# One transformer layer on one core: work moved at the seams of its four stages

## The chip, the cores and the metric

The kernel runs on one core of a Trainium2 chip. The metric is the device time of one launch in microseconds (us). The kernel before took 3391.18, 3396.15 and 3394.44 us in three runs, median 3394.44. The change is compared with it in the same way.

## The reference

Only the structure is shown; B = 2, S = 2048, D = 512, all float32.

```
x = x + LN(softmax(mask(LN(x) @ ctx.T / sqrt(512))) @ ctx) * gamma + beta     # ctx: 77 rows
y = LN(x)
src = rms(y + gqa(y)) * norm1       # 16 query heads, 4 key/value heads of 32, softmax over 2048 keys
src = src + moe(src)                # 8 experts, top 2, capacity 1280 rows, 512 -> 1024 -> gelu -> 512
out = x + rms(src) * norm2
```

## The kernel before

The 4096 rows are cut into 8 chunks of 512 rows (four tiles of 128). Four functions run one after the other, each with a block of its own; every engine ends its part before any starts the next block. Within a block each engine's instructions stand in a written order, and semaphores join them.

**Stage 1, `phase_project`.** For chunk c: layer norm of X, attention over ctx, x1 = X + that, y = LN(x1), then y transposed and projected to queries, keys and values. The chunks are staggered: while chunk c's attention runs, chunk c-1's y is transposed (`p_ps_t`, L559), split into a high part (ScalarE, `p_yTh`, L340) and a low part (VectorE, `p_yTl`, L482), and projected in six steps of twelve matmuls (L83 to L85). ScalarE takes each step's result as `p_hi` (L350) and VectorE as `p_lo` (L496). On VectorE `head_statistics(c + 2)` (four BATCH_NORM_STATS2, L399, four aggregates, L403, and the mask penalty `p_pen`, L415) stands at the end of `chunk(c)`, so `second_low(c)`, which makes `p_yTl`, comes behind it. GpSimd computes the reciprocal roots (L252, L254) and adds the rows `p_yb` (L277) and `p_xb` (L262).

**Stage 2, `phase_attend`.** 32 units (chunk, key/value head). A unit's keys and queries lie in `KS` and `QS`; for every unit the queries of the next chunk, the keys and the values are loaded. TensorE computes scores twice (once for the maxima, L1340, once transposed for the exponentials, L1354), GpSimd adds tiles of exponentials (L939, L943) so that fewer denominator matmuls (L1374) are needed. At the end of the last chunk its rows are projected, normalised (GpSimd L956, L951, then ScalarE L1095), transposed (L1392), routed to experts, and sent to `xe_d` by GpSimd's indirect DMAs (L1013).

**Stage 3, `phase_experts`.** SyncE loads an expert's w1 and w2 (into the space of `kept.x1`), ScalarE and VectorE split w1 into high and low parts (L1626, L1688), the rows' blocks are transposed (L1768) and go up and down. The results are added to `src_d` by indirect DMAs (L1610). At its end half of x1 is loaded.

**Stage 4, `phase_combine`.** Loads src and the rest of x1 on SyncE's queue. ScalarE sums squares (L1885), GpSimd makes the reciprocal root (L1870, L1872), VectorE multiplies (L1901, out of and into SBUF) and adds x1 (L1907); ScalarE stores `p_OUT` (L1878), of which there are two buffers.

Of the kernel before, what the change touches and what calls it, by code (L numbers as in the profile page):

```python
# [103 lines left out]
def phase_project(nc, x, ctx, mask, gamma, beta, qw, qb, kw, kb, vw, vb, ob, x1_d, y_d, qh_d, ql_d, kh_d, kl_d, v_d):  # L104
# [5 lines left out]
    with Scope(nc, "p1") as s:  # L110
# [283 lines left out]
        def _(dve):  # L394
# [104 lines left out]
            def chunk(c):  # L499
# [23 lines left out]
                if c + 2 < NC:  # L523
                    head_statistics(c + 2)
# [1430 lines left out]
```

## Time and profile before

| stretch | from, us | to, us |
|---|---|---|
| stage 1 | 0 | 341.1 |
| stage 2 | 341.1 | 2352.1 |
| stage 3 | 2352.1 | 3321.2 |
| stage 4 | 3321.2 | 3389.2 |

The profiled execution took 3391.0 us, its span is 3389.2 us. The ends of the stages are the first issues of SyncE in each block. In the whole span PE is busy 92%, DVE 63%, ACT 48%, POOL 60%, at a mean granted clock of 0.955; in stage 4 PE does nothing, and the sixteen DMA engines are busy 0.81 of the time. The shares of a whole span mix four stages that have different limits; what a change is worth is read in the stage that it touches, at the wait that ends last.

### The profile page before, as it was taken

The numbers are of one execution on the slowest core, as the hardware profiler recorded it, in microseconds if no ns is written. First come the engines' busy times: TensorE is split into PE (matmuls) and PEld (weight loads), VectorE is DVE, ScalarE is ACT, GpSimd is POOL, SyncE is SP. The second block draws the span as 40 slices with busy tenths as digits, with TensorE's granted clock in tenths as the row PEclk, the third lists the DMA queues.
The fourth block names the chain that finished last, engine by engine and source line by source line (L and its number), as shares of the span: only waits on it lengthen the run. The fifth ranks groups of instructions, "written<-read, shape, count | busy, mean of one in ns | idle before, by whom it ended". The sixth has DMA issues, their size and how long they took to land. (4 is left out here: it accounts for less than half of the span.)

```text
span 3389.2 us, 45574 instructions
## 1 busy us (share of the span) xinstructions
PE 3131.6 (92%) x16808; PEld 2017.8 (60%) x16808; DVE 2133.4 (63%) x3820; ACT 1616.5 (48%) x3252; POOL 2017.9 (60%) x856
## 2 busy tenths in 40 slices
PE   5888799999999999999999999983999999999990
PEld 4666444544544544544545445432999899989980
DVE  6765888878788788788788787822333333333325
ACT  2332166656566566556566565651333334333322
POOL 3332199889899899899899898993111111111112
PEclk7989599999999999999999999996999999999995
DMA  3544724212221313113122121002333333333237
GB/s 112 178 164 160 184 87 148 59 37 52 51 57 36 70 35 72 33 36 76 29 60 56 37 51 49 14 21 103 89 94 70 79 90 82 84 69 93 48 75 254
DMA packets 195376, 270.67 MB, mean 80 GB/s; under 512 B 80903, under 2 KB 86023, under 8 KB 192629
## 3 DMA queue, kind: packets, MB, share of 16 engines
q1 hardware_dynamic: 172864, 223.34, 22.9%
q0 software_dynamic: 16640, 35.42, 5.7%
q10 hardware_dynamic: 5685, 9.49, 0.8%
q8 instruction: 107, 1.75, 0.2%
q14 instruction: 80, 0.66, 0.1%
HBM read 152.98 MB, written 117.57 MB: 80 GB/s over the span
## 5 line engine op out<-in xcount | busy, mean ns | idle before, releaser
L1072 ACT ACTIVATE p_PR<-p_ps_b 128x512 f32<-128x512 f32 x2048 | 1066.1, 603 | 729.3 <-PE p_ps_b L1354 721.4
L1153 DVE TENSOR_REDUCE p_mxp<-p_ps_a 128x1 f32<-128x512 f32 x2048 | 1282.0, 681 | 209.3 <-PE p_ps_a L1340 198.6
L943 POOL TENSOR_TENSOR p_PP<-p_PP,p_PR 128x2048 f32<-128x2048 f32 x224 | 1027.5, 4587 | 38.2 <-ACT p_PR L1072 14.7
L1340 PE MATMUL p_ps_a<-p_KS,p_QS 96*128 96x512 f32 x2048 | 830.2, 437 | 36.3 <-DMA p_KS<-kh_d 15.9
L1354 PE MATMUL p_ps_b<-p_QS,p_KS 98*128 98x512 f32 x2048 | 755.7, 416 | 7.0 <-ACT p_PR L1072 6.0
L1340 PEld LDWEIGHTS p_ps_a<-p_KS,p_QS 96*128 96x128 f32 x2048 | 386.7, 192 | 472.8 <-DVE p_mxp L1153 325.2
L939 POOL TENSOR_TENSOR p_PP<-p_PR 128x2048 f32<-128x2048 f32 x128 | 587.0, 4586 | 96.3 <-ACT p_PR L1072 81.6
L1610 POOL DMA_INDIRECT src_d<-p_YE,p_token x80 | 123.9, 1548 | 836.9 <-DVE p_YE L1737 709.3
L1360 PE MATMUL p_ps_pv<-p_PR,p_VS 128*32 128x512 f32 x4096 | 511.3, 600 | 0.0
L1354 PEld LDWEIGHTS p_ps_b<-p_QS,p_KS 98*128 98x128 f32 x2048 | 387.4, 190 | 202.0 <-ACT p_PR L1072 117.5
L1655 ACT ACTIVATE p_hf<-p_ps_h 128x384 f32<-128x384 f32 (+1 forms) x256 | 112.0, 437 | 575.4 <-PE p_ps_h L85 569.4
L83 PE MATMUL p_ps_h<-p_xTh,p_w1h 128*128 128x256 f32 (+1 forms) x1024 | 323.6, 316 | 1.2 <-DVE p_xTl L1717 1.2
L85 PE MATMUL p_ps_h<-p_xTh,p_w1l 128*128 128x256 f32 (+1 forms) x1024 | 318.3, 311 | 0.0
L84 PE MATMUL p_ps_h<-p_xTl,p_w1h 128*128 128x256 f32 (+1 forms) x1024 | 318.1, 311 | 0.0
L1724 DVE TENSOR_TENSOR p_hl<-p_hf,p_hh 128x384 fp32r<-128x384 f32 (+1 forms) x256 | 126.1, 492 | 284.3 <-ACT p_hh L1659 284.3
L1737 DVE TENSOR_SCALAR p_YE<-p_ps_y,p_weight 128x512 f32<-128x512 f32 x80 | 60.0, 750 | 332.2 <-PE p_ps_y L85 278.6
L84 PE MATMUL p_ps_y<-p_w2l,p_hh 128*128 128x512 f32 x640 | 253.8, 397 | 0.0
L83 PE MATMUL p_ps_y<-p_w2h,p_hh 128*128 128x512 f32 x640 | 253.7, 396 | 0.0
L85 PE MATMUL p_ps_y<-p_w2h,p_hl 128*128 128x512 f32 x640 | 253.5, 396 | 0.0
L1360 PEld LDWEIGHTS p_ps_pv<-p_PR,p_VS 128*32 128x32 f32 x4096 | 99.8, 108 | 205.8 <-issue 113.0
L83 PEld LDWEIGHTS p_ps_h<-p_xTh,p_w1h 128*128 128x128 f32 x1024 | 193.2, 189 | 3.0 <-DVE p_xTl L1717 1.6
L84 PEld LDWEIGHTS p_ps_h<-p_xTl,p_w1h 128*128 128x128 f32 x1024 | 193.2, 189 | 1.3
(179 smaller groups left out, 3228.7 us busy)
## 6 DMA issues: line engine op xcount, KB each, us to landing
kept_x<-in_L_ffn_w SPq DMA_DIRECT2D x16, 2048.0 KB, 8.8
xe_d<-p_SR SPq DMA_DIRECT2D x20, 1056.0 KB, 9.5
p_QS<-qh_d SPq DMA_DIRECT2D x64, 256.0 KB, 3.9
p_KS<-kh_d SPq DMA_DIRECT2D x64, 256.0 KB, 6.7
p_XE<-xe_d SPq DMA_DIRECT2D x16, 792.0 KB, 7.1
src_d<-p_SR SPq DMA_DIRECT2D x9, 1024.0 KB, 10.1
p_XE<-xe_d SPq DMA_DIRECT2D x16, 528.0 KB, 3.6
p_X<-in_x SPq DMA_DIRECT2D x8, 1024.0 KB, 7.9
```

Of the source, the lines that this page charges most:

```text
L83: nc.tensor.matmul(out, ah, bh, start=start, stop=False)
L84: nc.tensor.matmul(out, ah, bl, start=False, stop=False)
L85: return nc.tensor.matmul(out, al, bh, start=False, stop=stop)
L939: nc.gpsimd.tensor_tensor(PP[:, buf, :, :], PR[:, tile_at(u, tile - 1), :, :], PR[:, tile_at(u, tile), :, :], ALU.add).then_inc(add_made, 1)
L943: nc.gpsimd.tensor_tensor(PP[:, buf, :, :], PP[:, buf, :, :], PR[:, tile_at(u, tile), :, :], ALU.add).then_inc(add_made, 1)
L1072: nc.scalar.activation(PR[:, tile_at(u, kt), j, :], ps_b[:, n % BK, :], ACT.Exp, scale=SCALE).then_inc(ex_made, 1)
L1153: nc.vector.reduce_max(mxp[:, a // (S // CH), a % (S // CH):a % (S // CH) + 1], ps_a[:, bank, :], AXX).then_inc(a_read, 1)
L1340: nc.tensor.matmul(ps_a[:, bank, :], QS[0:96, g, j, t * P:(t + 1) * P], KS[0:96, g, kb * CH:(kb + 1) * CH], start=True, stop=True).then_in ...
L1354: nc.tensor.matmul(ps_b[:, n % BK, :], KS[:, g, kt * P:(kt + 1) * P], QS[:, g, j, :], start=True, stop=True).then_inc(sc_mm, 1)
L1360: last = nc.tensor.matmul(ps_pv[HD * j:HD * (j + 1), :], VS[:, g, kt, :], PR[:, tile_at(u, kt), j, :], start=(kt == 0), stop=(kt == KT - 1))
L1610: nc.gpsimd.indirect_dma_start(out=src_rows, out_offset=bass.IndirectOffsetOnAxis(ap=token[:, b, t:t + 1].bitcast(U32), axis=0), in_=YE[:, ...
L1724: nc.vector.tensor_tensor(hl[:, b % 2, f, 0:n], hf[:, f % 2, 0:n], f32(hh[:, b % 2, f, 0:n]), ALU.subtract).then_inc(hl_made, 1)
```

## The change

Stage 1: `head_statistics(c + 1)` stands behind `second_low(c - 1)` at the start of `chunk(c)`, where `head_statistics(c + 2)` stood at the end. GpSimd's root for those rows moves with it to the head of its chunk. The transposes of y are issued in two halves with the probabilities' transposes between.

Stage 2: keys and values are loaded only when c is a multiple of 4 (a new batch). In the last unit the exponentials of tiles 13 to 15 are not added on GpSimd; each tile has its own denominator matmuls. The last chunk is normalised tile by tile: one root on GpSimd, one VectorE instruction. The space of `QS` and `KS` becomes a home for expert 0's w1, w2 and the split of w1, which are loaded and made at the end of stage 2.

Stage 3: the loads and the split of expert 0's w1 are gone from its start. At its end all eight chunks of x1 are loaded, the second half when the last up matmul is done.

Stage 4: no x1 load; chunk 0 in two pieces; norm_row is copied to PSUM; products of even tiles go to PSUM and are added by VectorE, those of odd tiles are added by GpSimd; results overwrite `SR` and are stored by SyncE, the last chunk in two stores.

The core of the diff:

```diff
@@ phase_project, vector
                 if c > 0:
                     second_low(c - 1)
+                    if c + 1 < NC:
+                        head_statistics(c + 1)
...
                 out(5)
-                if c + 2 < NC:
-                    head_statistics(c + 2)
@@ phase_project, tensor
                 if before:
-                    transposes(c - 1, y, y_made, y_tr, yl_made)
+                    transposes(c - 1, y, y_made, y_tr, yl_made, (0, 1))
                 probabilities(c, c == 0)
+                if before:
+                    transposes(c - 1, y, y_made, y_tr, yl_made, (2, 3))
@@ phase_attend, sync
+                if c % CB != 0:
+                    return
                 for part, src in ((0, kh_d), (1, kl_d), (2, kh_d)):
...
+            hold(sc_mm, NSC * NU)
+            sp.dma_start(kept.w1_raw[:], w1[0].rearrange("(k p) f -> p k f", p=P)).then_inc(kept.w1_in, 16)
+            sp.dma_start(kept.w2_raw[:], w2[0].rearrange("(k p) d -> p k d", p=P)).then_inc(kept.w2_in, 16)
             store_src(NC - 1)
@@ phase_attend, gpsimd
+                        if last and g == KV - 1 and ADDS[n][1] == NS - 1:
+                            continue
...
             for t in range(TT):
-                norm(NC - 1, t)
-            norm_power(NC - 1)
+                tile_power(t)
@@ phase_attend, scalar
-            for t in range(TT):
-                scale(NC - 1, t)
             sigmoid_exp(NC - 1)
+            act.wait_ge(kept.w1_in, 16)
+            for k in range(DK):
+                nc.scalar.activation(kept.w1h[:, k, :], kept.w1_raw[:, k, :], ACT.Copy).then_inc(kept.w1h_made, 1)
@@ phase_attend, vector
+            def normalise(c, t):
+                dve.wait_ge(rstd_made, c + t + 1)
+                nc.vector.scalar_tensor_tensor(SR[:, c % 2, t, 0:D], SR[:, c % 2, t, 0:D], sr_rstd[:, t:t + 1], norm_row[:],
+                                               ALU.mult, ALU.mult).then_inc(sr_made, 1)
...
             sum_chosen(NC - 1)
+            for k in range(DK):
+                dve.wait_ge(kept.w1h_made, k + 1)
+                nc.vector.tensor_tensor(kept.w1l[:, k, :], kept.w1_raw[:, k, :], f32(kept.w1h[:, k, :]), ALU.subtract).then_inc(kept.w1l_made, 1)
@@ phase_experts, sync
+            for c in range(NC):
+                if c == NC // 2:
+                    hold(sp, h_mm, FK * NB * E)
+                sp.dma_start(kept.x1(c), x1_d[c].rearrange("(t p) d -> p t d", p=P)).then_inc(kept.x1_in[2 * c // NC], 16)
@@ phase_combine, vector
+                    nc.vector.scalar_tensor_tensor(ps_n[:, even % NB, :] if t % 2 == 0 else SR[:, c, t, :], SR[:, c, t, :], rstd[:, c, t:t + 1], norm_ps[:],
                                                    ALU.mult, ALU.mult).then_inc(n_made, 1)
...
+                    nc.vector.tensor_tensor(SR[:, c, t, :], ps_n[:, (TT * c + t) // 2 % NB, :], kept.x1(c)[:, t, :], ALU.add).then_inc(even_made, 1)
```

How the instructions stand on VectorE in stage 1, where chunk 1 ends and chunk 2 begins, before (`p_yTl` is the low part of y, `p_stats<-p_X` the statistics of the rows ahead, `p_lo` the low part of a projection):

```order
L476 TENSOR_SCALAR p_y<-p_x,p_mv,p_rstd 128x512 x4
L496 SCALAR_TENSOR_TENSOR p_lo<-p_ps_pj,p_b_col,p_hi 128x512
L399 BN_STATS p_stats<-p_X 128x6 x4
L403 BN_AGGR p_mv<-p_stats 128x2 x4
L415 TENSOR_SCALAR p_pen<-p_MK 128x308
L482 TENSOR_TENSOR p_yTl<-p_ps_t,p_yTh 128x512 x4
L496 SCALAR_TENSOR_TENSOR p_lo<-p_ps_pj,p_b_col,p_hi 128x512
```

and now:

```order
L478 TENSOR_SCALAR p_y<-p_x,p_mv,p_rstd 128x512 x4
L498 SCALAR_TENSOR_TENSOR p_lo<-p_ps_pj,p_b_col,p_hi 128x512
L484 TENSOR_TENSOR p_yTl<-p_ps_t,p_yTh 128x512 x4
L401 BN_STATS p_stats<-p_X 128x6 x4
L405 BN_AGGR p_mv<-p_stats 128x2 x4
L417 TENSOR_SCALAR p_pen<-p_MK 128x308
L498 SCALAR_TENSOR_TENSOR p_lo<-p_ps_pj,p_b_col,p_hi 128x512
```

The nine instructions on the rows ahead went behind the four that make the low part.

TensorE at the end of stage 2's last unit, before (`p_ps_pv` are products with the values, `p_ps_den` the denominators, `p_PP` sums made by GpSimd, `p_PR` the exponentials themselves):

```order
L1374 MATMUL p_ps_den<-p_PP,p_ones 32x512 x4
L1360 MATMUL p_ps_pv<-p_PR,p_VS 32x512 x12
L1374 MATMUL p_ps_den<-p_PP,p_ones 32x512 x4
L83 MATMUL p_ps_a<-p_ow_hi,p_at_hi 128x512
L84 MATMUL p_ps_a<-p_ow_lo,p_at_hi 128x512
```

and now:

```order
L1410 MATMUL p_ps_den<-p_PP,p_ones 32x512 x4
L1396 MATMUL p_ps_pv<-p_PR,p_VS 32x512 x4
L1417 MATMUL p_ps_den<-p_PR,p_ones 32x512 x4
L1396 MATMUL p_ps_pv<-p_PR,p_VS 32x512 x4
L1417 MATMUL p_ps_den<-p_PR,p_ones 32x512 x4
L1396 MATMUL p_ps_pv<-p_PR,p_VS 32x512 x4
L1417 MATMUL p_ps_den<-p_PR,p_ones 32x512 x4
L83 MATMUL p_ps_a<-p_ow_hi,p_at_hi 128x512
```

One group of four denominator matmuls that read GpSimd's sum became three groups that read the exponentials.

VectorE at the end of stage 2, before (`p_chosen` is the last sum of the routing):

```order
L1245 COPY p_rk<-p_ps_a 128x64
L1249 TENSOR_REDUCE p_chosen<-p_prod 128x16
L58 UNCONDITIONAL_BRANCH
L1683 UNCONDITIONAL_BRANCH
L1688 TENSOR_TENSOR p_w1l<-kept_x,p_w1h 128x1024 x4
```

and now:

```order
L1271 COPY p_rk<-p_ps_a 128x64
L1275 TENSOR_REDUCE p_chosen<-p_prod 128x16
L1357 TENSOR_TENSOR home_w1l<-home_w_raw,home_w1h 128x1024 x4
L58 UNCONDITIONAL_BRANCH
L1721 UNCONDITIONAL_BRANCH
```

The four subtractions that make w1's low part went from behind the seam of the stages (the branches) to ahead of it, directly behind the last routing step.

## Rows read from the trace of the kernel before

**Rows 1.** Windows of stage 2's third chunk: busy time, clock, DMA share, GB/s.
```profile
871.00:1105.00 234.00, 231.70 (x1270) 116.55 (x1269) 190.03 (x322) 140.83 (x274) 216.43 (x77) 1.00 0.21 48
```

**Rows 2.** Timeline of DVE, stage 1: start, us, what, [idle before <-releaser].
```profile
169.34 0.75 DVE L496 SCALAR_TENSOR_TENSOR p_lo<-p_ps_pj,p_b_col,p_hi 128x512 fp32r<-128x512 f32 x1 [1.01 <-ACT p_hi L350]
...
173.12 1.28 DVE L482 TENSOR_TENSOR p_yTl<-p_ps_t,p_yTh 128x512 fp32r<-128x512 f32 x2
...
182.88 0.75 DVE L496 SCALAR_TENSOR_TENSOR p_lo<-p_ps_pj,p_b_col,p_hi 128x512 fp32r<-128x512 f32 x1 [6.26 <-ACT p_hi L350]
```

**Rows 3.** The same on DVE at the start of the last chunk.
```profile
282.11 0.75 DVE L496 SCALAR_TENSOR_TENSOR p_lo<-p_ps_pj,p_b_col,p_hi 128x512 fp32r<-128x512 f32 x1 [1.01 <-ACT p_hi L350]
...
290.32 0.75 DVE L496 SCALAR_TENSOR_TENSOR p_lo<-p_ps_pj,p_b_col,p_hi 128x512 fp32r<-128x512 f32 x1 [3.96 <-ACT p_hi L350]
```

**Rows 4.** Timeline of PE in the two stretches of rows 2 and 3.
```profile
173.86 1.40 PE L559 MATMUL p_ps_t<-p_ident,p_y 128*128 128x128 f32 x8 [4.11 <-DVE p_yTl L482]
...
177.26 0.63 PE L84 MATMUL p_ps_pj<-p_yTl,p_w_hi 128*128 128x512 f32 x1
...
283.75 1.25 PE L559 MATMUL p_ps_t<-p_ident,p_y 128*128 128x128 f32 x8 [1.23 <-DVE p_yTl L482]
...
286.99 0.39 PE L85 MATMUL p_ps_pj<-p_yTh,p_w_lo 128*128 128x512 f32 x1
```

**Rows 5.** Timeline of DVE where chunk 1 begins.
```profile
49.84 1.92 DVE L476 TENSOR_SCALAR p_y<-p_x,p_mv,p_rstd 128x512 f32<-128x512 f32 x4 [0.56 <-POOL p_rstd L254]
...
56.52 3.56 DVE L536 TENSOR_TENSOR p_w_lo<-p_w_raw,p_w_hi 128x768 fp32r<-128x768 f32 x4
```

**Rows 6.** Timeline of POOL beside DVE's instructions of rows 2.
```profile
179.44 4.97 POOL L262 TENSOR_TENSOR p_xb<-p_X,p_beta_row 128x512 f32<-128x512 f32 x4
```

**Rows 7.** Timeline of PE at the end of stage 2.
```profile
2283.01 1.07 PE L1374 MATMUL p_ps_den<-p_PP,p_ones 128*32 128x512 f32 x8 [1.78 <-POOL p_PP L943]
2283.89 2.76 PE L1360 MATMUL p_ps_pv<-p_PR,p_VS 128*32 128x512 f32 x24
2292.14 1.94 PE L1374 MATMUL p_ps_den<-p_PP,p_ones 128*32 128x512 f32 x8 [5.49 <-POOL p_PP L943]
...
2322.99 1.07 PE L1399 MATMUL p_ps_a<-p_srT,p_gw 128*32 128x512 f32 x8 [0.88 <-DVE p_srT L1199]
```

**Rows 8.** Timeline of ACT and POOL there.
```profile
2317.77 2.56 ACT L1095 ACTIVATE p_SR<-p_SR,p_sr_rstd 128x512 f32<-128x512 f32 x4 [2.78 <-POOL p_sr_rstd L951]
...
2334.00 0.20 POOL L995 TENSOR_TENSOR p_wt<-p_sigm,p_chosen 128x8 f32<-128x8 f32 x1 [0.40 <-DVE p_chosen L1249]
```

**Rows 9.** Timelines of DVE and PE at the start of stage 3.
```profile
2361.60 4.63 DVE L1688 TENSOR_TENSOR p_w1l<-kept_x,p_w1h 128x1024 fp32r<-128x1024 f32 x4 [27.69 <-ACT p_w1h L1626]
...
2362.67 1.51 PE L1768 MATMUL p_ps_t<-p_ident,p_XE 128*128 128x128 f32 x6 [32.64 <-DMA p_XE<-xe_d]
...
2369.89 0.69 PE L83 MATMUL p_ps_h<-p_xTh,p_w1h 128*128 128x384 f32 x1 [1.17 <-DVE p_xTl L1717]
```

**Rows 10.** Windows at the start of stage 3 and in stage 4.
```profile
2352.00:2357.00 5.00, 0.00 (x0) 0.00 (x0) 0.00 (x0) 0.00 (x0) 0.50 (x2) 0.50 0.77 256
...
3321.00:3326.00 5.00, 0.00 (x0) 0.00 (x0) 0.00 (x0) 0.00 (x0) 0.10 (x1) 0.50 0.64 234
3326.00:3331.00 5.00, 0.00 (x0) 0.00 (x0) 0.00 (x0) 3.82 (x11) 0.80 (x2) 0.50 1.00 374
...
3356.00:3361.00 5.00, 0.00 (x0) 0.00 (x0) 1.39 (x3) 2.89 (x8) 2.48 (x3) 0.50 1.05 410
```

**Rows 11.** Timeline of DVE and POOL in stage 4.
```profile
3331.56 2.74 DVE L1901 SCALAR_TENSOR_TENSOR p_OUT<-p_SR,p_rstd,kept_norm_row 128x512 f32<-128x512 f32 x4 [20.44 <-POOL p_rstd L1872]
3334.22 2.49 DVE L1907 TENSOR_TENSOR p_OUT<-p_OUT,kept_x 128x512 f32<-128x512 f32 x4
...
3333.77 3.80 POOL L1872 TENSOR_TENSOR p_rstd<-p_sv,p_half 128x4 f32<-128x4 f32 x1
3361.24 1.01 POOL L1872 TENSOR_TENSOR p_rstd<-p_sv,p_half 128x4 f32<-128x4 f32 x1
```

More of the change, by code:

```diff
@@ L551, in _, with transposes @@
             pe.wait_ge(ctx_t_made, 2)
-            def transposes(c, src, ready, done, evacuated):
+            def transposes(c, src, ready, done, evacuated, ks=range(DK)):
                 pe.wait_ge(ready, TT * c + TT)
-                for k in range(DK):
+                for k in ks:
                     if k >= 2:
@@ L686, in phase_attend @@
     NS = len(GROUPS)
+    assert D_LATE == 1 and GROUPS[-1] == tuple(range(KT - V_LATE, KT))
     ADDS = sorted((tiles[k], n, k) for n, tiles in enumerate(GROUPS) for k in range(1, len(tiles)))
@@ L1315, in _ @@
             low(NU - 1, KV - 1)
-            for t in range(TT):
-                project_out(NC - 1, t, (TAIL + t, (TAIL + t) % AK))
+            for t in range(TT + 1):
+                if t < TT:
+                    project_out(NC - 1, t, (TAIL + t, (TAIL + t) % AK))
+                if t > 0:
+                    normalise(NC - 1, t - 1)
             for t in range(TT):
@@ L1355, in scores, with loaded @@
                                  start=True, stop=True).then_inc(sc_mm, 1)
+            def loaded(c):
+                return 48 * (c + 1) + 48 * (c // CB + 1)
             def values(u, g, kt):
@@ L1376, in denominators, with tile_denominators @@
                 last.then_inc(den_mm, 1)
+            def tile_denominators(u, kt):
+                for j in range(G):
+                    last = nc.tensor.matmul(ps_den[HD * j:HD * (j + 1), :], ones[:, 0:HD], PR[:, tile_at(u, kt), j, :], start=False, stop=(kt == KT - 1))
+                if kt == KT - 1:
+                    last.then_inc(den_mm, 1)
             def project_out(c, t, at):
@@ L1491, in _ @@
                 values(NU - 1, KV - 1, kt)
-            for n in range(NS - D_LATE, NS):
-                denominators(NU - 1, n)
+                tile_denominators(NU - 1, kt)
             for t in range(TT):
@@ L1823, with __init__, x1, phase_combine @@
 class Kept:
-    def __init__(self, s):
-        self.norm_row = s.sb("norm_row", [P, D])
-        self.x1 = s.sb("x1", [P, PRE, TT, D])
-def phase_combine(nc, kept, src_d, x1_d, out):
-    norm_row = kept.norm_row
+    def __init__(self, nc, s):
+        with Scope(nc, "scores") as home:
+            self.QS = home.sb("QS", [98, KV, G, CH], F32R)
+            self.KS = home.sb("KS", [98, KV, S], F32R)
+        with Scope(nc, "rows") as home:
+            self.x1_rows = home.sb("x1", [P, NC, TT, D])
+        self.w1_raw = s.sb("w1_raw", [P, DK, F])
+        self.w2_raw = s.sb("w2_raw", [P, F // P, D])
+        self.w1h = s.sb("w1h", [P, DK, F], F32R)
+        self.w1l = s.sb("w1l", [P, DK, F], F32R)
+        self.w1_in, self.w2_in, self.w1h_made, self.w1l_made = (s.sem(n) for n in ("w1_in", "w2_in", "w1h_made", "w1l_made"))
+        self.x1_in = [s.sem(f"x1_in{i}") for i in range(2)]
+    def x1(self, c):
+        return self.x1_rows[:, c]
+def phase_combine(nc, kept, norm_row, src_d, out):
+    PIECES = [(0, 0, 2), (0, 2, 2)] + [(c, 0, TT) for c in range(1, NC)]
+    STORES = PIECES[:-1] + [(NC - 1, 0, 2), (NC - 1, 2, 2)]
+    NB = 4
     with Scope(nc, "p4") as s:
@@ L1928, in build_layer @@
                   x1_d, y_d, qh_d, ql_d, kh_d, kl_d, v_d)
-    phase_attend(nc, y_d, qh_d, ql_d, kh_d, kl_d, v_d, ow, norm1, gate_w, src_d, xe_d)
-    with Scope(nc, "kept") as s:
-        kept = Kept(s)
-        phase_experts(nc, xe_d, w1, w2, kept, src_rows, x1_d, norm2)
-        phase_combine(nc, kept, src_d, x1_d, chunks(out))
+    with Scope(nc, "home") as h:
+        kept = Kept(nc, h)
+        phase_attend(nc, y_d, qh_d, ql_d, kh_d, kl_d, v_d, ow, norm1, gate_w, src_d, xe_d, kept, w1, w2)
+        with Scope(nc, "kept") as s:
+            norm_row, norm_in = s.sb("norm_row", [P, D]), s.sem("norm_in")
+            phase_experts(nc, xe_d, w1, w2, kept, src_rows, x1_d, norm2, norm_row, norm_in)
+            phase_combine(nc, kept, norm_row, src_d, chunks(out))
 INPUTS = ["x", "ctx_1024", "mask_BxSxS2_ik1", "L0_xattn_gamma", "L0_xattn_beta", "L0_ffn_qw", "L0_ffn_qb", "L0_ffn_kw",
```

139 lines of the change are left out of this document (69 added, 70 removed).

## The prediction

> **What bounds the kernel now.** I read the windows of the four stages first, then the timeline at each seam, one engine after another. In the middle of stage 2 TensorE is busy 231.70 of 234.00 us of a chunk [rows 1]; it can give back little, and the change removes no TensorE work there. The idle time is elsewhere. In stage 1 VectorE's low part of y stands behind the statistics, and TensorE waits for it. At the end of stage 2 one row of work goes through POOL, DVE, ACT and PE in turn. At the start of stage 3 TensorE waits for rows and weights. In stage 4 the DMA engines carry 410 GB/s at a share of 1.05 [rows 10].
>
> **Stage 1, statistics moved.** The reader is to compare two chunk starts of the kernel before. From the start of the last `p_lo` of one chunk's projection to the first `p_lo` of the next it takes 182.88 - 169.34 = 13.54 us [rows 2]. At the last chunk no statistics stand between (there are no rows ahead), and the same stretch takes 290.32 - 282.11 = 8.21 us [rows 3]. So the trace of before holds the change already: 5.33 us. Of this 3.0 are the statistics (from the end of `p_lo`, 170.09, to 173.12); the other 2.3 are the clock. With them TensorE waits 4.11 us, then a projection matmul takes 0.63 us, the level of 1.2 GHz; without them it waits 1.23 us and one takes 0.39, that of 2.4 GHz [rows 4]. The statistics move to a place where VectorE idles 3.96 us even in the short form [rows 3], behind the low part; they are 3.0 us long, so they are hidden with 0.9 to spare. If POOL's additions hold the mask's instruction up, that cover is nearly gone, at about 1 us a chunk; POOL's root for the rows ahead is ready before its use, since its additions start earlier too. Chunks 2 to 6 gain 5 x 5.33 = 26.7. At chunk 1 the low part of y stands behind statistics and the weights' split: the split can start at 51.76 instead of 56.52 [rows 5], 4.8 us, at the low clock either way. Transposing y in halves moves nothing that is late: the third transpose still waits for the first low part. Sum 31.4; bounds 18 (only the statistics' own 3.0 come back, six times) and 32.
>
> **Stage 2, keys and values that stay.** 6 of 8 chunks load no keys or values. TensorE's rest in a chunk is 234.00 - 231.70 = 2.3 us [rows 1], so the gain lies between 0 and 6 x 2.3 = 14; the DMA share there is 0.21, far from full, and I take 0.
>
> **Stage 2, its end.** Before, the last denominators wait for two additions of POOL and run from 2292.14 to 2294.08. Now three tiles' values (2.76 us) alternate with three groups of denominator matmuls (0.88 each, from the start at 2283.01 to the next at 2283.89): 2283.89 + 2.76 + 2.7 = 2289.4, which is 4.7 us earlier [rows 7]. Normalising by tiles puts one VectorE product of 0.7 behind the last root, where ScalarE's four in a row took 2.56 [rows 8]: 1.9. And POOL no longer multiplies by norm_row ahead of its root, about the 1.24 of an addition [rows 6]. That is 3.1; I take 2.9, since VectorE's copies for the transposes now stand behind its last product (bounds 1 and 4). Both end in the matmul at 2322.99 [rows 7], which then starts near 2315.4: 7.6 us. Against this stands a new collision. The four subtractions for w1's low part, 4.63 us in one run [rows 9], now come directly behind `p_chosen` on VectorE, 0.1 us ahead of POOL's `p_wt` [rows 8], and everything that POOL still has to do (six small instructions, then eight sends) is queued behind `p_wt`. Stage 4 shows what such a run does: a root of POOL that takes 1.01 alone took 3.80 and ended 0.86 after the end of a run of four VectorE additions with both operands in SBUF [rows 11]. So I charge the run's whole length, 4.6. Net 3.0; bounds 1 and 7.6.
> The Trainium skill ("SBUF — State Buffer", Who interferes with whom) says that a VectorE instruction with two SBUF inputs and a GpSimd instruction that reads SBUF exclude each other, each for the whole instruction. By that rule read literally, POOL would get in after the first subtraction and the charge would be about a quarter of mine; that is a rival below.
>
> **Stage 3, its start.** Before, the first transpose is at 2362.67, 10.6 us after the block's start at 2352.1, since 2 MB of w1 stand ahead of the rows; the first up matmul follows 7.2 later at 2369.89 [rows 9], behind ScalarE's and VectorE's split of w1 (DVE from 2361.60 to 2366.23) [rows 9]. Now the rows are first in the queue. The first 5 us of the block moved 256 GB/s, 1.3 MB, though they hold the queue's start [rows 10]; the rows are 0.8 MB. I take 4.8 us to their landing (bounds 3.5 and 7). Without the split in between I take 4.8 from first transpose to first up matmul, since of the 7.2 some 2.5 are the wait for VectorE. 17.8 - 9.6 = 8.2 us; bounds 5.5 and 9.5. The hidden rows' ScalarE chain moves with it: w2 is there already and its split follows as before.
>
> **Stage 3, its end.** 4.2 MB of x1 are loaded beside the last four additions to src. They are done long before the last of these; nothing waits for them. 0, at most 1 lost.
>
> **Stage 4.** It lasts 3389.2 - 3321.2 = 68.0. It moves 20 x 1.05 = 21 MB now, and 16.8 after. The first 5 us move 234 GB/s, so about 2.3 are a start; loads alone then run at 374, loads beside stores at 410 [rows 10]. Loads: 8.4 MB at 374 = 22.4. Stores, on the same queue behind them: 8.4 MB at 405 = 20.7. With 2.3 at the start and 1.3 for the last landing this is 46.7. Is VectorE ready by then? It makes 32 products and 16 additions (before 32 and 32): 0.67 us [rows 11] x 48 = 32, with bounds of 0.60 and 0.75, from about 7 us on: 39 to 43, just under. POOL makes 16 additions of 1.24 (4.97 for four, rows 6) and nine pairs for the root of 1.3: 32 us, in the same time. Both fit if they do not hold each other up. Rows 6 speak for that: the four additions from 179.44 take 4.97 though VectorE works on `p_lo` with an operand in PSUM inside them, at 182.88 [rows 2]. Every VectorE instruction of the new stage has such an operand. Gain 68.0 - 46.7 = 21.3; bounds 14 (VectorE at 0.75 and every load seen late) and 24.
>
> **Sum.** 31.4 + 0 + 3.0 + 8.2 + 0 + 21.3 = 63.9 us. The profiled execution took 3391.0, so this one would take 3327.1. The median of the runs, 3394.4, lies 3.4 higher: 3330.5.
>
> **Rivals.** (a) The clock falls all the same at the chunk starts. For: the gap only has to be a little longer, as with 4.11 us, and POOL now adds beside VectorE's work. Against: the last chunk, where it stays. It costs 2.3 a chunk, six times, 13.8: 3344. Chance 0.14.
> (b) In stage 4 VectorE and POOL exclude each other although one operand is in PSUM. For: the row of 3.80 [rows 11]. Against: rows 6. Then they work one after the other, 32 + 32 + 7 = 71 us and 3 for the last store, 74 instead of 46.7: 3358. Chance 0.08.
> (c) The lock lasts one instruction, 1.2 us, and not the run of four, 4.6. For: it is a single row that shows more. That gives 3.4 back: 3327. Chance 0.10. The rule quoted above from the Trainium skill's "SBUF — State Buffer" is this case; the row of 3.80 speaks against it.
> (d) Slower than before: stage 2's tiles all lie elsewhere in SBUF now, and TensorE has 1% of slack there [rows 1]. If its matmuls took longer by their operands' place, each of the 32 units (58.5 us) would pay; from 2.0 us a unit on the whole gain of 63.9 is gone, and 2.5 give 3411. No row shows any such dependence. Chance 0.02.
> (e) That keys and values which stay give nothing is part of my forecast; if they did give the 14 us: 3317. Chance 0.05.
>
> **How the numbers follow.** The forecast, 3330.5, has the remaining 0.61, with a range of its own of 3321 to 3341. To hold 8 in 10 the range must take in (a) and (c), and the terms' lower bounds together (18 + 1 + 5.5 + 14, some 3356) need not all fall at once: 3318 to 3350 leaves out (b), (d), most of (e) and tails, under 0.2. This kernel's measurement tells 0.2%, 7 us, from no change. All cases but (d) and a remainder of 0.01 for what I have not seen are faster by more: faster 0.97, same 0.01, slower 0.02.
>
> **What would show it.** In the timeline of stage 1 the stretch from `p_lo` to `p_lo` over a chunk start is 8.2 us in chunks 2 to 7, a chunk is 32.3 instead of 37.6, and the projection's matmuls take 0.39 at once; stage 1 ends near 310. A stretch of 10.5 with matmuls of 0.63 means rival (a). A unit of stage 2 stays at 58.5; longer is (d), shorter (e). POOL's `p_wt` takes or waits 4 us while w1's low part is made; if it does not, (c). In stage 3 the first transpose comes about 5 us after the block's start. Stage 4 takes 47 us with a DMA share near 1 until the last stores; if POOL's additions take far over 1.24 each, (b). The prediction is wrong in its core if stage 1 ends later than 325 or stage 4 lasts over 55 us.

## The result and the profile after

The changed kernel takes 3332.86 us (median of four runs, 3331.54 to 3333.35), the kernel before 3393.89 beside it: a ratio of 0.982, 95% interval 0.9803 to 0.9837, 61.0 us less. The forecast was 3330.5 with a range of 3318 to 3350. The profiled execution took 3333.35, with a span of 3331.6 and a mean granted clock of 0.969. The table is made from two single profiles, and the one of before (3391.0 us) is as short as its shortest run, that of the changed kernel is of its longest, so its differences add up to 57.6 and not to 61.0.

| length, us | before | after | difference | predicted |
|---|---|---|---|---|
| stage 1 | 341.1 | 313.7 | -27.4 | -31.4 |
| stage 2 | 2011.0 | 2007.7 | -3.3 | -3.0 |
| stage 3 | 969.1 | 964.1 | -5.0 | -8.2 |
| stage 4 | 68.0 | 46.2 | -21.9 | -21.3 |

Two rows of the table are off by more than a microsecond, stage 1 and stage 3. The near agreement of stage 2 is partly luck, as shown below. I begin with what VectorE does at a chunk start in stage 1, the same place as [rows 2]. Columns of a timeline: start, duration of the group, engine, line, what, [idle before <- releaser].

```profile
157.88 0.75 DVE L498 SCALAR_TENSOR_TENSOR p_lo<-p_ps_pj,p_b_col,p_hi 128x512 fp32r<-128x512 f32 x1 [1.00 <-ACT p_hi L350]
158.78 1.29 DVE L484 TENSOR_TENSOR p_yTl<-p_ps_t,p_yTh 128x512 fp32r<-128x512 f32 x2 [0.15 <-ACT p_yTh L340]
160.98 1.29 DVE L484 TENSOR_TENSOR p_yTl<-p_ps_t,p_yTh 128x512 fp32r<-128x512 f32 x2 [0.91 <-ACT p_yTh L340]
162.18 2.46 DVE L401 BATCH_NORM_STATS2 p_stats<-p_X 128x6 f32<-128x512 f32 x4
164.79 0.38 DVE L405 BATCH_NORM_AGGREGATE p_mv<-p_stats 128x2 f32<-128x6 f32 x4
165.09 0.83 DVE L417 TENSOR_SCALAR p_pen<-p_MK 128x308 f32<-128x308 int32 x1
166.23 0.75 DVE L498 SCALAR_TENSOR_TENSOR p_lo<-p_ps_pj,p_b_col,p_hi 128x512 fp32r<-128x512 f32 x1 [0.32 <-ACT p_hi L350]
```

From `p_lo` to `p_lo` it is 8.35 us; 8.2 was predicted, 13.54 was before. The statistics lie where VectorE idled, with 0.32 left of the 0.9: `p_pen` takes 0.83 here, where GpSimd's `p_xb` runs beside it, and took 0.29 before. The four statistics beside the same additions take 2.46, as before. TensorE there, to be set beside [rows 4]:

```profile
162.32 0.50 PE L83 MATMUL p_ps_pj<-p_yTh,p_w_hi 128*128 128x512 f32 x1 [1.54 <-DVE p_yTl L484]
162.66 0.39 PE L84 MATMUL p_ps_pj<-p_yTl,p_w_hi 128*128 128x512 f32 x1
```

The matmuls are at 0.39 at once, as predicted. The pitch of a chunk (from one chunk start to the next) is 32.4 (37.6 before). At chunk 1 the weights' split now starts 1.83 after `p_y` (6.68 before [rows 5]): 4.85 gained. So the stage should be 31 shorter, and is 27.4, because the profiled execution began slower: its 32 logits matmuls (chunk 0, scores over ctx) at 19.20 took 7.11 us (3.80 before), and `p_y` of chunk 0 came 3.75 later. The likely cause is the low clock, but this is read from the lengths alone: the granted clock reads 1.00 over the logits in both profiles, and it also reads 1.00 at 63.7 of this one, where a projection matmul takes 0.63, so the column decides nothing at the start of a profile. In 9 of the 14 profiles of this study these matmuls took 7.11, in 5 they took 3.80, whatever the kernel; with the statistics in their new place the low part of y for chunk 0 starts near 58.9 in the one kind and near 55.6 in the other.

TensorE at the end of the last unit of stage 2, which answers to [rows 7], one line of each kind:

```profile
2256.55 1.06 PE L1410 MATMUL p_ps_den<-p_PP,p_ones 128*32 128x512 f32 x8 [0.60 <-POOL p_PP L954]
2257.43 1.04 PE L1396 MATMUL p_ps_pv<-p_PR,p_VS 128*32 128x512 f32 x8
...
2261.72 1.04 PE L1417 MATMUL p_ps_den<-p_PR,p_ones 128*32 128x512 f32 x8
```

From the first denominators to the end of the last are 6.2 us, 11.1 before: 4.9 gained. From the stage's start to `p_chosen` it takes 1985.8 us, against 1992.5: 6.7 gained. But the last unit alone, from the start of these denominators to `p_chosen`, went from 50.6 us to 42.9: 7.7 gained, for the 7.6 predicted. The missing 1.0 was lost ahead of it, in the part of stage 2 for which no gain or loss was forecast; from profile to profile the stretch from the stage's start to `p_chosen` lies between 1982.6 and 1986.6 in the kernels with this end. Then comes the collision, in the timelines of VectorE and GpSimd, where [rows 8] show 0.20 for `p_wt`:

```profile
2299.49 0.29 DVE L1275 TENSOR_REDUCE p_chosen<-p_prod 128x16 f32<-128x128 f32 x1 [3.36 <-POOL p_prod L1005]
2299.69 4.63 DVE L1357 TENSOR_TENSOR home_w1l<-home_w_raw,home_w1h 128x1024 fp32r<-128x1024 f32 x4
```
```profile
2299.85 1.12 POOL L1014 TENSOR_TENSOR p_wt<-p_sigm,p_chosen 128x8 f32<-128x8 f32 x1 [0.40 <-DVE p_chosen L1275]
2301.05 1.05 POOL L1015 TENSOR_SCALAR p_far<-p_chosen 128x8 f32<-128x8 f32 x1
2302.18 1.09 POOL L1016 TENSOR_SCALAR p_SR<-p_token 128x4 f32<-128x4 f32 x1
2303.36 1.03 POOL L1018 TENSOR_TENSOR p_SR<-p_wt,p_wsum 128x8 f32<-128x8 f32 x1
2304.34 0.20 POOL L1021 TENSOR_TENSOR p_place<-p_chosen,p_far 128x8 f32<-128x8 f32 x1
...
2305.80 1.11 POOL L1032 DMA_INDIRECT xe_d<-p_SR,p_places  x1 [0.89 <-POOL p_places L1024]
```

The run of four does not lock GpSimd out as a whole. Each of four GpSimd instructions takes about as long as one subtraction (1.16 us each), as if it waited for one, and the two that are left take 0.20 and 0.19. The price is 4.29 - 0.84 = 3.45 us.

TensorE at the start of stage 3, 4.54 and 9.3 us after its start at 2321.39 (10.6 and 17.8 before, [rows 9]):

```profile
2325.93 1.51 PE L1805 MATMUL p_ps_t<-p_ident,p_XE 128*128 128x128 f32 x6 [30.07 <-DMA p_XE<-xe_d]
...
2330.70 0.69 PE L83 MATMUL p_ps_h<-p_xTh,home_w1h 128*128 128x384 f32 x1 [1.17 <-DVE p_xTl L1755]
```

That is 8.5 gained, yet the stage is only 5.0 shorter. The loss is at its end, in GpSimd's last four additions to src. Before, they started 5.62 us apart (3295.12, 3300.75, 3306.37, 3311.99). Now:

```profile
3256.14 1.54 POOL L1649 DMA_INDIRECT src_d<-p_YE,p_token  x1 [15.59 <-DVE p_YE L1775]
3264.86 1.54 POOL L1649 DMA_INDIRECT src_d<-p_YE,p_token  x1 [7.17 <-DMA src_d<-p_YE,p_token]
3270.46 1.54 POOL L1649 DMA_INDIRECT src_d<-p_YE,p_token  x1 [4.06 <-DMA src_d<-p_YE,p_token]
3276.05 1.54 POOL L1649 DMA_INDIRECT src_d<-p_YE,p_token  x1 [4.04 <-DMA src_d<-p_YE,p_token]
```

The second waits 7.17 us for the landing of the first, which shares the DMA engines with 4.2 MB of x1 (the window 3256 to 3261 has a DMA share of 1.05). The step 8.72 is 3.1 longer than the others, and the chain never catches up. The first of the four comes 8.3 earlier in the stage than before, the last 5.2 earlier.

Stage 4 is one window; columns: stretch, length, busy time of PE, PEld, DVE, ACT, POOL with instruction counts, clock, DMA share, GB/s.

```profile
3285.45:3331.60 46.15, 0.00 (x0) 0.00 (x0) 30.82 (x48) 23.72 (x65) 30.16 (x35) 0.50 0.98 364
```

It takes 46.15 us (46.7 predicted). VectorE runs from 3299.08 to its end at 3325.98 without a rest, at 3.83 a chunk, and the chain of waits that ended last goes through it and, in the last chunk, through GpSimd's additions. The DMA share is 1.04 in the same time. Which of the two bounds can't be read from this window; the run without computation (e7) settles it.

### The profile page after: what moved, and what is told of

Same layout as the page of the kernel before. It is cut to its first block and busy times, and to the rows that moved or that the text cites. A ratio compares the mean times of both kernels' runs of the same rounds, so it can differ in the third digit from the quotient of the medians.

```text
span 3331.6 us, 45551 instructions
## 1 busy us (share of the span) xinstructions
PE 3128.2 (94%) x16824; PEld 2014.9 (60%) x16824; DVE 2129.1 (64%) x3808; ACT 1614.5 (48%) x3249; POOL 2019.4 (61%) x874
## 3 DMA queue, kind: packets, MB, share of 16 engines
q10 hardware_dynamic: 1461, 1.11, 0.1%
## 5 line engine op out<-in xcount | busy, mean ns | idle before, releaser
L1372 PE MATMUL p_ps_a<-scores_KS,scores_QS 96*128 96x512 f32 x2048 | 831.5, 438 | 35.6 <-DMA scores_KS<-kh_d 15.5
L1386 PE MATMUL p_ps_b<-scores_QS,scores_KS 98*128 98x512 f32 x2048 | 756.6, 417 | 6.6 <-ACT p_PR L1092 5.7
L1372 PEld LDWEIGHTS p_ps_a<-scores_KS,scores_QS 96*128 96x128 f32 x2048 | 387.4, 193 | 472.3 <-DVE p_mxp L1174 326.1
L1386 PEld LDWEIGHTS p_ps_b<-scores_QS,scores_KS 98*128 98x128 f32 x2048 | 388.6, 190 | 201.7 <-ACT p_PR L1092 117.1
L83 PE MATMUL p_ps_h<-p_xTh,home_w1h 128*128 128x256 f32 (+1 forms) x1024 | 323.8, 316 | 1.2 <-DVE p_xTl L1755 1.2
L85 PE MATMUL p_ps_h<-p_xTh,home_w1l 128*128 128x256 f32 (+1 forms) x1024 | 318.3, 311 | 0.0
L84 PE MATMUL p_ps_h<-p_xTl,home_w1h 128*128 128x256 f32 (+1 forms) x1024 | 318.1, 311 | 0.0
L83 PEld LDWEIGHTS p_ps_h<-p_xTh,home_w1h 128*128 128x128 f32 x1024 | 193.2, 189 | 3.0 <-DVE p_xTl L1755 1.6
L84 PEld LDWEIGHTS p_ps_h<-p_xTl,home_w1h 128*128 128x128 f32 x1024 | 193.3, 189 | 1.3
```

What stands on the lines that cost most here:

```text
L83: nc.tensor.matmul(out, ah, bh, start=start, stop=False)
L84: nc.tensor.matmul(out, ah, bl, start=False, stop=False)
L85: return nc.tensor.matmul(out, al, bh, start=False, stop=stop)
L1372: nc.tensor.matmul(ps_a[:, bank, :], QS[0:96, g, j, t * P:(t + 1) * P], KS[0:96, g, kb * CH:(kb + 1) * CH], start=True, stop=True).then_in ...
L1386: nc.tensor.matmul(ps_b[:, n % BK, :], KS[:, g, kt * P:(kt + 1) * P], QS[:, g, j, :], start=True, stop=True).then_inc(sc_mm, 1)
```

## The experiments

Each kernel is the changed one with one edit. Totals are medians; the runs of one kernel lie 1.4 to 7.4 us apart, so small effects are read from stretches of the traces. Where an edit left a stage alone, its length was 2004.5 to 2008.6 in stage 2, 963.3 to 965.2 in stage 3 and 45.7 to 47.2 in stage 4. `...` marks lines left out of an edit.

**The statistics moved back (e1).**

```diff
                     second_low(c - 1)
-                    if c + 1 < NC:
-                        head_statistics(c + 1)
...
                 out(5)
+                if c + 2 < NC:
+                    head_statistics(c + 2)
```

> The changed kernel with only the statistics of the rows ahead (VectorE) and their root (GpSimd) where they stood before, at the end of a chunk. My theory (the order on VectorE, 4.8 at chunk 1 and 5.3 at each of five chunks): stage 1 is 31 us longer, so 3364; p_lo to p_lo over a chunk start is 13.5 us again and the first projection matmuls take 0.63. Rival (the gain of stage 1 is of several origins, the split transposes of y among them): under 25 us of it come back, under 3358. Rival (only the 3.0 us of the statistics count, the clock follows something else): 18 us, 3351.

Measured: 3362.46 us (3362.11 to 3363.5), 29.6 more than the changed kernel (3332.86, and 3333.15 when it was run again). The pitch is 37.5 instead of 32.4, and the split of the weights starts 6.67 after `p_y` instead of 1.83. 5 x 5.1 + 4.8 = 30.3, and stage 1 lasts 343.9 against 313.7, both with logits of 7.11. TensorE at the chunk start:

```profile
179.97 0.79 PE L83 MATMUL p_ps_pj<-p_yTh,p_w_hi 128*128 128x512 f32 x1 [1.41 <-DVE p_yTl L484]
180.56 0.63 PE L84 MATMUL p_ps_pj<-p_yTl,p_w_hi 128*128 128x512 f32 x1
```

The place of the statistics (on VectorE, with their root on GpSimd) is the whole gain of stage 1; both rivals fall.

**TensorE kept at work during the wait (e12).** It is e1 with a filler.

```diff
+                if c > 1:
+                    pe.wait_ge(pj_out, NM * (c - 1))
+                    for i in range(16):
+                        nc.tensor.matmul(ps_pj[:, 1, :], w_hi[:, 0, 0:P], w_hi[:, 1, 0:CH], start=True, stop=True)
                 probabilities(c, c == 0)
```

> The kernel of e1 with sixteen matmuls more at each chunk start from the third on: TensorE multiplies two pieces of the weights into a PSUM bank that nothing reads, while it waits for the low part of y. They end about when the wait ends. The predicted split of 5.3 into 3.0 for the statistics and 2.3 for the clock: the projection's matmuls stay at 0.39, a stretch from p_lo to p_lo is 11.2 instead of 13.5, stage 1 is 6 x 2.3 = 14 us shorter than in e1, 3350. Rival (the clock falls whatever TensorE does there, or the 2.3 are not the clock's): stretch 13.5, as e1, 3364. Rival (the filler itself is in the way): longer than e1.

TensorE in e12 at a chunk start:

```profile
167.50 3.96 PE L623 MATMUL p_ps_pj<-p_w_hi 128*128 128x512 f32 x16 [0.38 <-DVE p_lo L498]
171.30 0.60 PE L587 MATMUL p_ps_pt<-p_ident,p_pr 128*77 128x128 f32 x4
171.74 1.04 PE L561 MATMUL p_ps_t<-p_ident,p_y 128*128 128x128 f32 x8
174.41 0.50 PE L83 MATMUL p_ps_pj<-p_yTh,p_w_hi 128*128 128x512 f32 x1 [1.63 <-DVE p_yTl L484]
174.74 0.40 PE L84 MATMUL p_ps_pj<-p_yTl,p_w_hi 128*128 128x512 f32 x1
```

With TensorE busy the projection runs at 0.40, the level of 2.4 GHz (granted clock 1.00 from 175 to 180; 0.50 from 181 to 184 in e1), although VectorE is as late as in e1. Measured: 3355.66 us (3353.67 to 3356.25), 6.8 less than e1; the pitch is 35.66 against 37.5. So of the 5.1 us of a chunk 1.8 are the clock's and 3.3 the order's (2.3 and 3.0 predicted). The total is short of the 14 because only five chunk starts gain (9.3 together) and the last, which had no gap, loses 3.3 to the filler; 6.0 is what is left. The profiled run of e12 also had the short logits and that of e1 the long ones, so only the stretches behind the start are compared. The mechanism holds, the size was too large.

**y in one piece (e2).**

```diff
...
-                    transposes(c - 1, y, y_made, y_tr, yl_made, (0, 1))
+                    transposes(c - 1, y, y_made, y_tr, yl_made)
                 probabilities(c, c == 0)
-                if before:
-                    transposes(c - 1, y, y_made, y_tr, yl_made, (2, 3))
```

> The changed kernel with y transposed and taken by ScalarE in one piece, ahead of the probabilities, as before. My theory (the halves move nothing that is late): chunk period 32.4 as in the changed kernel, 3333 within 3 us. Rival (the halves let TensorE work inside its wait, and keep the gap short): a gap of more than 1.5 us opens before the third transpose, matmuls at 0.63 appear, up to 2.3 a chunk, 14 us: 3347.

Measured: 3328.84 us (3327.48 to 3333.27). The pitch is 32.27 instead of 32.38; the halves cost 0.1 a chunk, and the rival falls. That makes 0.6 of the 4.0. The profiled run also began with logits of 3.80; how much of the rest belongs to the edit, through the clock at single chunk starts, is open (e13).

**Keys and values loaded again (e3).**

```diff
-                if c % CB != 0:
-                    return
...
```

> The changed kernel with keys and values loaded for every unit again, as before. My theory (they were never late and the DMA engines are a fifth busy there): stage 2 stays at 2007.7 us within 1.5, total 3333. Rival (the loads held TensorE up by waits or by shared access to SBUF): up to 14 us longer, 3347. The DMA share of a chunk in the middle goes from 0.11 back to 0.21 in either case.

The same window of stage 2 in the changed kernel and in e3; the last two columns are the DMA share and GB/s:

```profile
839.00:1073.00 234.00, 231.75 (x1269) 116.47 (x1268) 189.50 (x321) 140.91 (x275) 216.61 (x76) 1.00 0.11 33
```
```profile
839.00:1073.00 234.00, 231.68 (x1269) 116.45 (x1268) 189.52 (x321) 140.90 (x275) 216.43 (x76) 1.00 0.22 51
```

Measured: 3334.15 us (3332.5 to 3335.24); stage 2 took 2006.1. Twice the traffic, and TensorE does not notice: 231.68 us of 234.00 are busy against 231.75. The keys that stay are worth nothing that shows within the spread of the stage.

**The denominators by GpSimd again (e10).**

```diff
...
             for kt in range(KT - V_LATE, KT):
                 values(NU - 1, KV - 1, kt)
-                tile_denominators(NU - 1, kt)
+            denominators(NU - 1, NS - 1)
```

> The changed kernel with GpSimd's two additions for the last group of exponentials and one group of four denominator matmuls behind all values, as before, at the end of the last unit. Prediction's term: the denominators end 4.7 us later, and with them everything to p_chosen; stage 2 is 4.7 longer, 3337.6. Rival (GpSimd's additions were ready sooner here, or the chain behind takes part of it up): 2 or less.

Measured: 3337.64 us (3336.23 to 3339.46), 4.5 more than the changed kernel in the same series (3333.15, below). TensorE waits 5.49 for GpSimd's sum, as before, and ends 11.1 after the first group instead of 6.2.

**w1's low part later (e4).**

```diff
             sum_chosen(NC - 1)
+            dve.wait_ge(placed, PLACED * NC)
             for k in range(DK):
```

> The changed kernel in which VectorE waits, before the four subtractions for w1's low part at the end of stage 2, until GpSimd has done its last small instruction. In the changed kernel four of GpSimd's six took 1.03 to 1.12 instead of 0.2, and the first send came 6.02 after p_chosen (2.57 before). My theory after the result (each subtraction excludes GpSimd for its own length, and each time GpSimd gets one instruction in between): the six take 0.2 to 0.3 each again, the send comes 2.6 after p_chosen, stage 2 is 3.4 shorter, 3329.5 from 3332.9; the subtractions run beside the sends and cost nothing. The prediction's own figure (the run of four locks as one): 4.6. Rival (c) of the prediction (one instruction): 1.2. Rival (the subtractions now hold the sends up, or end the stage): no gain, 3333 or more.

Measured: 3332.31 us (3331.57 to 3333.45), a total that tells nothing. GpSimd in e4:

```profile
2299.31 0.21 POOL L1014 TENSOR_TENSOR p_wt<-p_sigm,p_chosen 128x8 f32<-128x8 f32 x1 [0.40 <-DVE p_chosen L1275]
...
2301.81 1.35 POOL L1032 DMA_INDIRECT xe_d<-p_SR,p_places  x1 [0.89 <-POOL p_places L1024]
2303.47 1.83 POOL L1032 DMA_INDIRECT xe_d<-p_SR,p_places  x1 [0.30 <-issue]
2305.61 0.97 POOL L1032 DMA_INDIRECT xe_d<-p_SR,p_places  x1 [0.31 <-issue]
```

The small instructions are short again, so the subtractions were the cause. But now the first two sends, which GpSimd prepares beside the subtractions, take 1.35 and 1.83 instead of 1.11 and 0.98. The stretch from `p_chosen` to the start of stage 3 is the measure: 21.88 to 21.92 in eleven profiles with the subtractions at once, 19.56 here, 18.46 before. So 3.44 was lost and 2.34 come back. My expectation of 3.4 was wrong by the sends.

**The rows behind 2 MB (e9).**

```diff
+            sp.dma_start(w1_raw, w1_v[0:1].rearrange("a p k f -> p (a k) f")).then_inc(fill_in, 16)
             load_block(0, 0)
...
```

> The changed kernel with one more load of 2 MB ahead of the rows in SyncE's queue at the start of stage 3 (it writes w1's second expert into the space of w1_raw, where nothing reads it before it is loaded again); the early split of w1 stays. This is the part of stage 3's start that is the order of the queue. Prediction: rows landed 4.8 after the start instead of 10.6, so 5.8 longer, 3338.7; the other 2.4 of the 8.2 are the split and stay gained. Rival (the rows wait for something else at the start, or 2 MB cost their 5.6 only in part since queues share): 3 or less, 3336.

Measured: 3339.63 us (3338.43 to 3340.55), 6.5 more. SyncE's first issue is at 2322.22 and the first transpose at 2332.23, 10.0 later instead of 4.54: the queue's order is 5.5 of the 8.5 us. The first up matmul still follows 4.8 behind the transpose, where it was 7.2 before: 2.4, the share that was given to the split. The other 0.6 stays open.

**The last x1 loads behind the additions (e5).**

```diff
                 if c == NC // 2:
                     hold(sp, h_mm, FK * NB * E)
+                if c == NC - 2:
+                    sp.wait_ge(y_added, 16 * NT * E)
```

> The changed kernel in which the last two of the four x1 loads that follow the last up matmul wait until the last rows are added to src. In the changed kernel all four run beside the first of the last four additions, whose landing then takes 8.7 us instead of 5.6, and everything behind it in this chain is 3.0 later. My theory (the chain of additions has no slack, a load beside one delays the end of the stage by what it takes from it): all additions follow at 5.6, the last lands 3 us earlier; the two late loads of 2.1 MB take 5.6 us and reach 1 to 2 us into stage 4, so 1 to 2 us remain, 3331.5. Rival (the 3 us come from something else, the token lists or GpSimd): additions as in the changed kernel, and stage 4 later, 3334.

GpSimd's additions in e5:

```profile
3254.19 1.54 POOL L1651 DMA_INDIRECT src_d<-p_YE,p_token  x1 [15.59 <-DVE p_YE L1777]
3259.81 1.54 POOL L1651 DMA_INDIRECT src_d<-p_YE,p_token  x1 [4.08 <-DMA src_d<-p_YE,p_token]
3265.43 1.54 POOL L1651 DMA_INDIRECT src_d<-p_YE,p_token  x1 [4.08 <-DVE p_YE L1777]
3271.05 1.54 POOL L1651 DMA_INDIRECT src_d<-p_YE,p_token  x1 [4.08 <-DVE p_YE L1777]
```

All steps are 5.62. Stage 3 took 960.9 (963.3 to 965.2 elsewhere): 3.2 gained. Stage 4 took 46.98, which is 0.8 more, but inside the 45.7 to 47.2 of the other profiles. The total, 3332.16 (3328.86 to 3336.22), is too spread to show it. The traffic beside the chain of additions is the cause of the 3 us.

**Stage 4 without its computation (e7).** The stores wait for the landings alone.

```diff
-                sp.wait_ge(even_made, (TT * c + t + n) // 2)
-                sp.wait_ge(odd_made, (TT * c + t + n) // 2)
+                sp.wait_ge(sr_in[min(STORES.index((c, t, n)), len(PIECES) - 1)], 16)
...
```

> The changed kernel with the computation of the last stage left out (no squares, roots, products or additions): each piece of src is stored as soon as it has landed. It leaves the output without its last normalising and residual. The prediction (stage 4 is the DMA engines' loads plus stores: 2.3 + 22.4 + 20.7 + 1.3): 46.2 as in the changed kernel, within 1 us, 3333. Rival (VectorE's chain bounds: first landing, then 3.83 a chunk without a rest, then the last store): without it the stage falls to the sum of the transfers alone, 44 or less, 3330 or less.

```profile
3282.12:3328.40 46.28, 0.00 (x0) 0.00 (x0) 0.00 (x0) 0.60 (x1) 0.10 (x1) 0.50 0.97 363
```

46.28 us with nothing computed, 46.15 with everything (total 3334.12, 3330.17 to 3335.77): the 44 or less of the rival is not there. The stage is its transfers; the chain of waits through VectorE runs just inside them.

**Weights' row from SBUF (e8).**

```diff
-                    nc.vector.scalar_tensor_tensor(ps_n[:, even % NB, :] if t % 2 == 0 else SR[:, c, t, :], SR[:, c, t, :], rstd[:, c, t:t + 1], norm_ps[:],
+                    nc.vector.scalar_tensor_tensor(ps_n[:, even % NB, :] if t % 2 == 0 else SR[:, c, t, :], SR[:, c, t, :], rstd[:, c, t:t + 1], norm_row[:],
```

> The changed kernel with the products of stage 4 reading the row of weights from SBUF instead of its copy in PSUM, so that 32 VectorE instructions have two operands in SBUF. Theory (such an instruction and GpSimd exclude each other for its length): VectorE's 32 x 0.67 = 21.4 us and GpSimd's 30 us no longer overlap; the 16 additions of VectorE still do. The stage ends when 21.4 + 30 and the 7 at its start are over, 58 + 3 for the store = 61 instead of 46: 3348. Rival (b turned round: there is no exclusion, the row of 3.80 was something else): 3333.

One chunk of it, VectorE and GpSimd (in the changed kernel these take 0.75, 0.74, 0.75, 0.74 and 0.20, 1.02, 2.49):

```profile
3303.60 0.89 DVE L1960 SCALAR_TENSOR_TENSOR p_ps_n<-p_SR,p_rstd,kept_norm_row 128x512 f32<-128x512 f32 x1
3304.41 1.75 DVE L1960 SCALAR_TENSOR_TENSOR p_SR<-p_SR,p_rstd,kept_norm_row 128x512 f32<-128x512 f32 x1
3306.08 0.75 DVE L1960 SCALAR_TENSOR_TENSOR p_ps_n<-p_SR,p_rstd,kept_norm_row 128x512 f32<-128x512 f32 x1
3306.74 0.74 DVE L1960 SCALAR_TENSOR_TENSOR p_SR<-p_SR,p_rstd,kept_norm_row 128x512 f32<-128x512 f32 x1
```
```profile
3302.67 2.94 POOL L1932 TENSOR_TENSOR p_SR<-p_SR,rows_x 128x512 f32<-128x512 f32 x2
3305.69 0.52 POOL L1923 TENSOR_SCALAR p_sv<-p_ss 128x4 f32<-128x4 f32 x1
3306.29 1.40 POOL L1925 TENSOR_TENSOR p_rstd<-p_sv,p_half 128x4 f32<-128x4 f32 x1
```

Measured: 3340.84 us (3339.45 to 3342.47), the stage 53.3 instead of 46.15. The exclusion is real, and the copy in PSUM is what keeps it out: a chunk takes 5.0 instead of 3.83 on VectorE. But it costs 7.2, not 15. The two engines take turns by instruction, and not everything is held: the product that takes 1.0 longer is the one that meets the end of GpSimd's additions, while two others take their 0.75 and 0.74 beside a root (which takes 1.40 instead of 1.02). I had added both engines' whole times.

**The changed kernel again (e13).**

> The changed kernel itself once more, word for word, on the chip and beside the runs of e11, so that differences of 2 to 6 us can be told: 3331 to 3336. If the clock is still low when the first logits run at the start (7.1 us instead of 3.8 for 32 small matmuls), the profiled run is 3.3 longer than where it is not.

Measured: 3333.15 us (3331.59 to 3337.86), before 3395.14 beside it. Its profile, of the longest of these runs, shows what the spread is made of. Its logits took 7.11, as in the first profile of this kernel, so the 3.3 of the expectation can't be seen between these two; over all profiles `p_y` of chunk 0 starts at 50.2 to 50.7 with the short logits and at 53.3 to 53.8 with the long ones. Stage 1 ends at 317.97, 4.3 later than in the first profile, since three of the chunk starts look like this on TensorE:

```profile
163.97 0.57 PE L83 MATMUL p_ps_pj<-p_yTh,p_w_hi 128*128 128x512 f32 x1 [1.53 <-DVE p_yTl L484]
164.33 0.63 PE L84 MATMUL p_ps_pj<-p_yTl,p_w_hi 128*128 128x512 f32 x1
```

The pitch is 33.95 there and 32.38 at the others. That is rival (a) in part of the executions: the same program, the same wait of 1.53, and the clock falls (granted clock 0.57 from 164 to 168) or does not. In nine profiles with y in halves and the statistics in their new place the first matmuls were slow at 11 of 54 chunk starts behind the first; in e2 and e11, with y in one piece and a wait of 0.98, at none of 12. That the one piece protects from it is suggested by this, not shown.

**The gains joined (e11).** y in one piece, the x1 loads of e5, and the subtractions at the head of stage 3:

```diff
...
+            split_w1(0)
             rows_low(0, 0, range(DK))
```

> The changed kernel with y taken in one piece (as e2), the last two x1 loads behind the additions (as e5), and the four subtractions for w1's low part at the head of stage 3, where VectorE has nothing to do until the rows' first transposes. Expected from the parts: stage 2 is 3.4 shorter (GpSimd's small instructions at 0.2, sends at 1.28 from the first), the first transpose of stage 3 still 4.5 after the block's start and the first up matmul 4.8 behind it; 2.3 from the end of stage 3 and start of stage 4 together as e5 showed; 0.7 from stage 1. Sum 6.4: 3326.5 if the same kernel without these stands at 3332.9. Rival (the subtractions push the low part of the rows back, or GpSimd's identity behind them pushes the first transpose): up to 4.6 of it back, 3331.

Measured in one series: 3326.89 us (3321.86 to 3328.77) against 3333.15 for the changed kernel, 0.9793 of before (0.9780 to 0.9807). The sends are 1.28 apart and 18.46 us lie between `p_chosen` and stage 3, all 3.44 regained. The one loss is at the start of stage 3, where the first transpose comes 5.5 after the start and not 4.54, with the subtractions beside the rows' landing. Stage 4 took 47.3, 1.2 more, just above the 45.7 to 47.2. Each of its five runs is shorter than each of the five of the changed kernel beside it (3331.59 and more): it beats both kernels. The 6.3 gained for 6.4 expected are an agreement of sums only, since single runs are spread as widely.

## Why the prediction was right, and where not

- **Stage 1, statistics moved: 31.4.** Right in mechanism and nearly in size: e1 gives 29.6 in the totals and 30.3 in stage 1. The split was 3.3 order and 1.8 clock instead of 3.0 and 2.3. The profile's 27.4 is short through the slow start, which I had not thought to vary. Transposing in halves was put at nothing; it costs 0.1 a chunk. Rival (a) had a chance of 0.14 as something that happens at all chunk starts or at none; it happens at one in five.
- **Keys and values that stay: 0.** Right (e3).
- **Stage 2's end: 7.6 gained.** 7.7 in the last unit, 6.7 counted from the stage's start. The denominators gave 4.9 for 4.7 (e10). From the reciprocal at 2262.83 to `p_chosen` the rest gave 2.8 for 2.9, although the router's matmuls at 2287.73 took 1.93 at a granted clock of 0.50 (1.07 at 1.00 before). No run takes the tile by tile normalising back, so its 2.8 rest on this comparison alone. The net of stage 2, -3.3 for -3.0, is near by luck: 1.2 too much was charged for the collision, and 1.0 was lost ahead of the last unit.
- **The collision: 4.6.** Right place, wrong law and size. "Stage 4 shows what such a run does" generalised one row of a root. Measured 3.44: one subtraction for each GpSimd instruction that meets the run. Rival (c) had the law but counted one instruction where four stood in the queue. The rule of the Trainium skill ("SBUF — State Buffer", Who interferes with whom), exclusion for each whole instruction, agrees with these four rows. The step that failed is the charge of the run's length in [rows 11]; 3.44 lies between the 1.2 and the 4.6.
- **Stage 3's start: 8.2.** 8.5, of which 5.5 are the queue (e9).
- **Stage 3's end: "0, at most 1 lost".** Wrong: 3.0 lost. I asked whether anything waits for the loads, not who shares the engines with them. The additions form a chain in which each waits for the last one's landing, at 5.6 a step, the same as TensorE's step; what delays one, delays the end (e5). Of the stage's 5.0, 8.5 - 3.0 = 5.5 are explained. The other 0.5 went in two places, 0.2 between the first up matmul and the first of the four additions and 0.2 behind the last; why is open, and the stage varies by 1.9 from profile to profile.
- **Stage 4: 46.7 by the sum of transfers.** 46.15, and 46.28 without computation (e7). VectorE was "just under", and it is. Rival (b) would have been so with the row in SBUF, but at 53, not 74 (e8).

So the total, 61.0 for a forecast of 63.9, was right because its two large terms were. That the 3 us lost at stage 3's end are about the whole difference is partly luck: stage 1 gave about 1 less than forecast and stage 2 lost 1.0 ahead of its last unit, while the collision cost 1.2 less and stage 4 gave 0.5 more, and the runs of one kernel lie microseconds apart.

## What to carry to other kernels

A move that opens a gap is best looked for in the kernel's own trace at a place where the moved work is absent, as at the last chunk here: it gives order and clock together. Of work moved beside a chain, ask what it shares with the chain (DMA engines, SBUF), not only who waits for it. A small instruction behind a long run of another engine's can cost one of that run's instructions, and so can each one queued after it. Before two profiles are compared stage by stage, look at how far profiles of one and the same kernel lie apart; here that was 6 us in stage 1 and 4 in stage 2.

## What the runs showed of the hardware

- VectorE subtractions with two SBUF operands (1.16 us each) stretched four GpSimd instructions of 0.2 us to between 1.03 and 1.12 each, one for one. Indirect sends beside them took up to 1.83 instead of 0.98.
- A VectorE instruction with one SBUF operand was held too, and another was not: `p_pen` takes 0.83 beside GpSimd's `p_xb` and 0.29 elsewhere (e12), the four statistics 2.46 with and without it.
- GpSimd's root took 3.80 beside four VectorE additions [rows 11] but 1.40 beside two products (e8); why is open.
- An indirect addition of 128 rows started a next one 5.6 us later alone and 8.7 beside plain loads (383 GB/s in all).
- The length of the first matmuls after launch (3.80 or 7.11 for 32) and at single chunk starts (0.40 or 0.63) differs between executions of one program: 3.3 and 1.6 us each time. At the chunk starts the granted clock shows it (1.00 or 0.5 to 0.6); at launch it does not.
